# One activation-table step a group instead of two, in a fused Mamba and tree-FFN kernel on one core

## The reference

```python
h = layernorm(x) * (1 + ca) + sa
xp, z = split(h @ W_in)                     # 256 channels each
u = silu(causal_conv4(xp) + conv_b)
dt_r, Bm, Cm = split(u @ W_xp)              # 8, 16, 16
delta = softplus(dt_r @ W_dt + dt_bias)
# for each of the 16 states n:  h_t = exp(delta_t * A_n) * h_(t-1) + delta_t * B_tn * u_t
# y_t = sum over n of C_tn * h_t
y = (y + u * D_skip) * silu(z)
x = x + ga * (y @ W_out)
h = layernorm(x) * (1 + cb) + sb
gate = sigmoid((h @ Wq.T) @ routers.T)      # 255 nodes of a tree of depth 8
leaf_prob = products of gate and 1 - gate along each path   # 256 leaves
x = x + gb * ((leaf_prob @ leaf_values) @ Wout_w.T + Wout_b)
```

## Time and profile before

| | |
|---|---|
| median of 3 runs | 538.68 us (534.51 to 538.88) |
| profiled execution, its own time | 538.69 us |
| its span, first to last instruction | 536.9 us |
| outside the span | 1.79 us |
| busy: DVE, POOL, PE, ACT | 454.3, 445.3, 406.6, 374.1 us |
| granted TensorE clock, mean | 0.898 of full |

### The profile page before, as it was taken

How to read it: one execution, slowest core, us unless ns; L and a number is a source line. 1 busy time by engine, 2 the same in 40 slices (tenths; PEclk the granted TensorE clock), 3 DMA queues, 4 the chain that set the end, 5 groups by cost and what they waited for, 6 DMA issues and landing times. The chain is left out here.

```text
span 536.9 us, 6647 instructions
## 1 busy us (share of the span) xinstructions
PE 406.6 (76%) x2104; PEld 278.4 (52%) x2135; DVE 454.3 (85%) x542; ACT 374.1 (70%) x680; POOL 445.3 (83%) x246
## 2 busy tenths in 40 slices
PE   8978834896679757984899747984899758574887
PEld 4436524483548435663567435662557435464554
DVE  6788794998999968998799968997899968998871
ACT  3367774478966888588756898598856886448454
POOL 3468889999899978997799979997889978998800
PEclk8989885899799969998799979999899969785899
DMA  6491062200721073303512063303512063300001
GB/s 169 132 357 75 6 235 89 106 2 21 249 106 62 6 236 117 99 0 125 208 34 89 5 236 117 100 1 131 202 43 81 6 234 118 98 0 2 8 13 39
DMA packets 24867, 53.16 MB, mean 99 GB/s; under 512 B 4601, under 2 KB 13952, under 8 KB 20736
## 3 DMA queue, kind: packets, MB, share of 16 engines
q1 hardware_dynamic: 24832, 52.74, 29.0%
HBM read 50.11 MB, written 2.62 MB: 98 GB/s over the span
## 5 line engine op out<-in xcount | busy, mean ns | idle before, releaser
L561 POOL TENSOR_TENSOR hc<-h,c_rows 128x1024 f32<-128x1024 f32 x126 | 296.6, 2367 | 41.4 <-DVE h L1286 38.0
L1286 DVE TENSOR_TENSOR_SCAN h<-dA,state,dbu 128x512 f32<-128x512 f32 x192 | 234.6, 1270 | 20.1 <-ACT dA L649 19.8
L649 ACT ACTIVATE dA<-delta,a_neg 128x512 f32<-128x512 f32 x256 | 173.1, 684 | 44.5 <-DVE h L1286 43.6
L1065 PE MATMUL yb<-ident,hc 128*128 128x128 f32 x1024 | 155.8, 291 | 22.0 <-POOL hc L561 20.1
L1065 PEld LDWEIGHTS yb<-ident,hc 128*128 128x128 f32 x1024 | 133.3, 152 | 64.7 <-issue 32.4
L548 POOL TENSOR_TENSOR dbu<-du,b_rows 128x1024 f32<-128x1024 f32 x48 | 113.4, 2363 | 4.0 <-DMA b_rows<-bc_dram 4.0
L1299 DVE TENSOR_TENSOR dbu<-du,bb 128x1024 f32<-128x1024 f32 x80 | 96.5, 1206 | 20.5 <-PE bb L1090 10.9
L1286 DVE TENSOR_TENSOR_SCAN h<-dA,dbu 128x512 f32<-128x512 f32 x64 | 74.6, 1210 | 17.8 <-ACT dA L649 17.7
L973 PE MATMUL mf<-f_hT,w_conv 128*128 128x512 f32 x112 | 56.1, 628 | 2.0 <-ACT zu L708 1.4
L996 PE MATMUL mf<-zu,w_xdt 128*128 128x512 f32 x56 | 31.2, 640 | 17.1 <-ACT delta L742 11.5
L824 PE MATMUL mt<-ident,t_xhat 128*128 128x128 f32 x28 | 7.6, 427 | 37.8 <-ACT t_xhat L590 37.8
(11 more groups left out here) (198 smaller groups left out, 544.5 us busy)
## 6 DMA issues: line engine op xcount, KB each, us to landing
c_rows<-bc_dram SPq DMA_DIRECT2D x32, 1024.0 KB, 6.8
b_rows<-bc_dram SPq DMA_DIRECT2D x48, 256.0 KB, 7.3
xs<-in_L_attn_x_dram SPq DMA_DIRECT2D x8, 256.0 KB, 3.8
out_dram<-xs SPq DMA_DIRECT2D x7, 256.0 KB, 5.6
ygT<-in_L_attn_conv_w_dram SPq DMA_DIRECT2D x1, 512.0 KB, 5.1
bc_dram<-xd SPq DMA_DIRECT2D x8, 64.0 KB, 1.6
probT<-in_L_wmod_dram SPq DMA_DIRECT2D x1, 384.0 KB, 4.0
w_in<-in_L_attn_W_in_dram SPq DMA_DIRECT2D x1, 256.0 KB, 4.2
```

Of the source, the lines that this page charges most:

```text
L561: nc.gpsimd.tensor_tensor(hc[:, pair % RC, :, :], h[:, pair % RH, :, :], c_rows[:, q, n % NQ, :].unsqueeze(1).broadcast_to([P, HALVES, T]) ...
L649: nc.scalar.activation(dA[ke % RD][:, :], delta[:, ge % 2, half, :], ACT.Exp, scale=a_neg[:, half, n:n + 1]).then_inc(s_dA, 1)
L1065: last = nc.tensor.matmul(bank[:, tile], hc[:, pair % RC, half, tile], ident[:, :], start=False, stop=n == N - 1, is_transpose=True, skip_ ...
L1286: v.tensor_tensor_scan(h[:, pair % RH, half, :], dA[k % RD][:, :], dbu[:, pair % RW, half, :], start, ALU.mult, ALU.add).then_inc(s_scan, 1)
```

## The change

ACT has one table step a group, at F_TABLES = 10: silu table, silu of u and z, softplus table, softplus of the nodes (groups with a leaf part) and of delta, exp table. Delta's softplus reads the two products right from PSUM, with the bias, in two instructions of 512; the two copies with bias (L742) are gone. So that both products can wait to be read, the second goes to the bank `mt` (the "t" side of JOBS), between the output product and the leaf sums. Statistics of the next front come at step 12 beside those of the tail; the steps of the tail, the leaf part, du and the B parts are moved; in group 0 the tail weights are turned, multiplied and taken out by step 9.

```diff
--- before.py
+++ after.py
@@ -81,26 +81,27 @@
 
 
 
-    N_STATS, N_RSTD, N_OFF, N_XHAT = 19, 21, 22, 25
-    F_SILU, F_DT, F_SP, F_DU = 10, (13, 15), 17, (25, 26)
-    F_HI, F_R1, F_MID, F_R2, F_LO = 21, 22, 23, 24, 25
-    T_GATE, T_ADD, T_STATS, T_RSTD, T_OFF, T_XHAT = (4, 5), 12, 12, 15, 16, 19
-    U_FIN = 28
+    N_STATS, N_RSTD, N_OFF, N_XHAT = 12, 16, 17, 20
+    F_TABLES, F_DU = 10, (21, 22)
+    F_HI, F_R1, F_MID, F_R2, F_LO = 18, 19, 20, 21, 22
+    T_GATE, T_ADD, T_STATS, T_RSTD, T_OFF, T_XHAT = (4, 5), 12, 12, 13, 14, 18
+    U_FIN = 20
 
 
 
 
     JOBS = {
         "f": {("xp", 0): (1, (0, 1)), ("xp", 1): (1, (3, 4)), ("z", 0): (1, (7,)), ("z", 1): (1, (8,)),
-              ("dt", 0): (1, (11, 12)), ("dt", 1): (1, (13, 14)), ("xd", 0): (1, (15, 16)), ("tr", 0): (2, (28,))},
-        "t": {("yt", 0): (-1, (6,)), ("yt", 1): (-1, (8,)), ("out", 0): (-1, (10,)), ("tr", 0): (-1, (20,)),
-              ("lp", 0): (-2, (22,)), ("lp", 1): (-2, (24,)), ("ff", 0): (-2, (25, 26)), ("node", 0): (-1, (28,)),
-              ("node", 1): (-1, (30,))},
+              ("dt", 0): (1, (11, 12)), ("xd", 0): (1, (15, 16)), ("tr", 0): (2, (26,))},
+        "t": {("yt", 0): (-1, (6,)), ("yt", 1): (-1, (8,)), ("out", 0): (-1, (10,)), ("dt", 1): (1, (13, 14)),
+              ("lp", 0): (-2, (15,)), ("lp", 1): (-2, (17,)), ("ff", 0): (-2, (19, 20)), ("tr", 0): (-1, (22,)),
+              ("node", 0): (-1, (25,)), ("node", 1): (-1, (27,))},
     }
     BY_DVE = {"out", "ff"}
+    FIRST_BY_HAND = {("f", "xp"): 1, ("f", "dt"): 1, ("t", "dt"): 1, ("f", "xd"): 1, ("f", "tr"): 2}
     Z_OF_0 = (29, 30)
     TR_OF_1 = STEPS - 1
-    W_TURN, W_COPY, W_MUL, W_TAKE, W_SCALE = (4, 9), (7, 11), 13, 16, 20
+    W_TURN, W_COPY, W_MUL, W_TAKE, W_SCALE = (2, 5), (4, 7), 8, 9, 20
 
     WARM_START = 9
     WARM_XHAT = 3
@@ -110,8 +111,7 @@
     for side in JOBS:
         for g in range(FIRST, LAST + 1):
             for (name, part), (off, steps) in sorted(JOBS[side].items(), key=lambda job: job[1][1]):
-                first = {"xp": 1, "dt": 1, "xd": 1, "tr": 2}.get(name, 0) if side == "f" else 0
-                if first <= g + off < GROUPS:
+                if FIRST_BY_HAND.get((side, name), 0) <= g + off < GROUPS:
                     job_at[side, name, part, g + off] = len(read_at[side])
                     by = "dve" if name in BY_DVE else "act"
                     reads[side, by] = reads.get((side, by), 0) + 1
@@ -337,6 +337,13 @@
             _, by, count = read_at[side][job_at[side, name, part, g]]
             eng.wait_ge(s_read[side, by], count)
 
+        def wait_delta(eng, g, half):
+
+            if g == 0:
+                eng.wait_ge((s_d0, s_delta)[half], 1)
+            else:
+                wait_read(eng, "ft"[half], "dt", half, g)
+
         def wait_bank(eng, side, n):
 
             if n >= RM[side]:
@@ -562,7 +569,7 @@
                                                 ALU.mult).then_inc(s_hc, 1)
                     if front and s in F_DU:
                         half = F_DU.index(s)
-                        pool.wait_ge(s_delta, f + 1)
+                        wait_delta(pool, f, half)
                         pool.wait_ge(s_silu, f + 1)
                         nc.gpsimd.tensor_tensor(du[:, f % 2, half, :], delta[:, f % 2, half, :],
                                                 zu[:, f % 2, HALVES + half, :], ALU.mult).then_inc(s_du, 1)
@@ -640,7 +647,7 @@
                         ge, se = divmod(ke, STEPS)
                         n, half = divmod(se, HALVES)
                         if se < HALVES:
-                            act.wait_ge(s_delta, ge + 1)
+                            wait_delta(act, ge, se)
                         if ke >= RD:
                             act.wait_ge(s_scan, ke - RD + 1)
                         if ke == 0:
@@ -707,7 +714,7 @@
                                 act.wait_ge(s_gate, HALVES * (f - 2) + half + 1)
                             nc.scalar.activation(zu[:, f % 2, half, :], job("f", "z", half, f)[1][:, :],
                                                  ACT.Copy).then_inc(s_read["f", "act"], 1)
-                    if front and s == F_SILU:
+                    if front and s == F_TABLES:
 
                         wait_read(act, "f", "xp", 1, f)
                         u_part = zu[:, f % 2, HALVES:, :]
@@ -716,6 +723,20 @@
                             wait_read(act, "f", "z", 1, fz)
                             z_part = zu[:, fz % 2, 0:HALVES, :]
                             nc.scalar.activation(z_part, z_part, ACT.Silu).then_inc(s_zsilu, 1)
+                    if (front or leaf) and s == F_TABLES:
+                        if leaf:
+
+                            wait_read(act, "t", "node", 1, u)
+                            if u:
+                                wait_job(act, "t", "lp", 1, u - 1)
+                            nc.scalar.activation(node_s[:, :, :], node_x[:, :, :], ACT.Softplus, scale=-1.0)
+                            nc.scalar.activation(node_x[:, :, :], node_x[:, :, :], ACT.Softplus).then_inc(s_nsp, 1)
+                        if front:
+                            for half in range(HALVES):
+                                side = "ft"[half]
+                                wait_job(act, side, "dt", half, f)
+                                nc.scalar.activation(delta[:, f % 2, half, :], job(side, "dt", half, f)[1][:, :],
+                                                     ACT.Softplus, bias=dtb[:, half:half + 1]).then_inc(s_read[side, "act"], 1)
                         nc.scalar.preload_act_table_set("natural_log_exp_and_others")
                     if front and s == read_step("f", "xd", 0):
                         wait_job(act, "f", "xd", 0, f)
@@ -736,25 +757,6 @@
                         act.wait_ge(s_r2, f + 1)
                         nc.scalar.activation(b_parts[B_LO:P, f % 2, :], xd_bank[B_LO:P, :],
                                              ACT.Copy).then_inc(s_lo, 1)
-                    if front and s in F_DT:
-                        half = F_DT.index(s)
-                        wait_job(act, "f", "dt", half, f)
-                        nc.scalar.activation(delta[:, f % 2, half, :], job("f", "dt", half, f)[1][:, :], ACT.Identity,
-                                             bias=dtb[:, half:half + 1]).then_inc(s_read["f", "act"], 1)
-                    if (front or leaf) and s == F_SP:
-                        if front:
-
-                            wait_read(act, "f", "dt", 1, f)
-                            both = delta[:, f % 2, :, :]
-                            nc.scalar.activation(both, both, ACT.Softplus).then_inc(s_delta, 1)
-                        if leaf:
-
-                            wait_read(act, "t", "node", 1, u)
-                            if u:
-                                wait_job(act, "t", "lp", 1, u - 1)
-                            nc.scalar.activation(node_s[:, :, :], node_x[:, :, :], ACT.Softplus, scale=-1.0)
-                            nc.scalar.activation(node_x[:, :, :], node_x[:, :, :], ACT.Softplus).then_inc(s_nsp, 1)
-                        nc.scalar.preload_act_table_set("natural_log_exp_and_others")
                     if tail and s == T_RSTD:
                         rstd(t, t_mv, t_rs, t_nm, s_tvar, s_trs)
                     if tail and s == T_XHAT:
@@ -993,6 +995,8 @@
 
                     if piece == 0:
                         pe.wait_ge(s_silu, g + 1)
+                        if (side, g) == ("t", 1):
+                            pe.wait_ge(s_wtake, 1)
                     last = nc.tensor.matmul(bank[:, :], w_xdt[:, piece, part * P:(part + 1) * P],
                                             zu[:, g % 2, HALVES + piece, :],
                                             start=piece == 0, stop=piece == HALVES - 1)
```

## The result

The changed kernel takes 546.65 us (median of 4 runs, 545.31 to 547.69); the kernel before took 538.36 beside it (534.51 to 538.88). The ratio is 1.0168, with an interval of 1.0116 to 1.0221: slower by 1.7%, just outside the range that was forecast. The profiled execution took 547.69 us, 545.9 of them span. In what follows medians are over all executions of a kernel but one, of `two_loads`, that took 986 us.

The account below looks back on a forecast made before the run. ACT's absences in other tables set the turn, by how far each outlasts what DVE has in hand. Group 0 +7.7, group 1 +1.8, five turns -5.2, the end -4.3 sum to 0.0: 538.7 us, range 529 to 546.

Parts of the forecast that it names:

- The turns, "-5.2": Five loop turns, 138.34 to 438.24 us: 26.3 us of DVE standing against 31.5, so 5.2 us less.
- Scan 13's standing: DVE waiting at scan 13 for ACT's one long absence: 4.1 us a turn, 5.4 in group 6.
- DVE's reserve: Group 5, during ACT's absence: exps in hand, residual and statistics keep DVE busy until 360.3, scan 13 starting at 364.4.
- The second term: Step 20: a new DVE wait for the leaf product, 0.9 us a turn, between none and 2.
- The third term: Behind the absence: DVE's waits for B rows and "remote", 10.0 us in five turns, taken as gone.
- the slower rival: Steps 13 to 20: late leaf product brings B-row waits back, 548.7 us; 0.30, shared with a start-up worse than priced.
- Group 0, "+7.7": Group 0: the longer absence delays POOL, full afterwards, its multiply moving from 61.36 to 69.0: 7.7 us lost, at least 4.3.
- the 1.8 us ahead of the load: Group 0: PE's weight products and three copies, now earlier, delay the silu load by an estimated 1.8 us.
- Group 1, "+1.8": Group 1: POOL stands 3.7 us at two multiplies, where it had 1.98: 1.8 us lost, between 0 and 2.5.
- From 438.24 on, "-4.3": Group 7 on: softplus step costs nothing and DVE's waits go: 4.3 us gained, between 1.4 and 6.0.
- The 6.28 us of group 0, "worth nothing": Group 0 at 87.92: DVE's longest wait goes with the earlier offset, but gains nothing since POOL is full there.
- ACT's 16 us, "none of it on the path by itself": ACT's spared loads (9.0 us) and copies (9.4 us) gain nothing by themselves, since ACT waits for DVE in the rest of a turn.

Follow-up runs that it names:

- two_loads: The changed kernel with two more table loads in the one table step, right after silu of z (14 loads in seven groups): 556.87 us, ratio 1.0306.
- after: The changed kernel itself, with nothing further edited: 546.65 us.
- ufin22: The changed kernel with DVE adding the leaf product (leaf residual) at step 22 in place of 20: 537.23 us, ratio 0.9984.
- before: The kernel without the change, run beside each other kernel: 538.36 us beside the changed kernel.
- after_paths: The changed kernel with POOL making the path matrices at the start of the program, not at step 20 of group 0: 540.06 us, ratio 1.0025.
- split_g0: The changed kernel with the table step cut in two in group 0 alone (silu at step 10, softplus at 15): 542.93 us, ratio 1.0085.
- ufin22_ring4: The changed kernel with leaf residual at step 22, a fourth exp buffer, in SBUF, and ACT three steps ahead: 580.65 us, ratio 1.0799.

## Why the prediction was wrong

**The turns, "-5.2": the step that failed.** It had three terms. Scan 13's standing was 4 x 4.1 + 5.4 = 21.8 and measured 24.8 (4.57, 4.55, 5.08, 4.72 and 5.90). The absence has the length I gave it: the scan comes 10.47 us after the silu load, against 10.5. DVE's reserve was a little too large.

The second term was 0.9 us a turn at step 20; it measured 2.1 in four turns and 0.4 in the last, 8.9 for 4.5. In group 5 DVE comes to step 20 23.6 us after the silu load (forecast 23.5), and ACT's second leaf exp is done after 21.7 (21.5): both as forecast. Mis-sized is the way from that exp to the finished product, 2.9 us in the forecast and 4.0 measured. I had PE's work in front of the product done by then, at the full clock. But PE has stood twice, its clock is at the lower level, the leaf sum takes 2.07 and 1.91 us, and the y_sum, fill and y_sum behind it are slow too; the product starts 1.3 us after the exp is done. In the kernel before that sum, in group 5, follows other work closely:

```profile
383.53 1.13 PE L949 MATMUL mt<-node_s,path 128*128 128x512 f32 x2 [0.21 <-ACT probT L781]
384.49 1.02 PE L950 MATMUL mt<-node_x,path 128*128 128x512 f32 x2
```

The last turn of after shows the other case in the same kernel. In group 6 the clock is back before the sum ends, the rows behind it have the full pace, and DVE waits 0.44 us, 2.85 after the exp is done:

```profile
447.82 0.60 PE L1069 MATMUL yb<-ident,hc 128*128 128x128 f32 x4
448.26 0.38 PE L1094 MATMUL bb<-b_parts,sel 128*128 128x512 bf16 x1
448.47 0.60 PE L1069 MATMUL yb<-ident,hc 128*128 128x128 f32 x4
```

```profile
448.32 0.58 ACT L783 ACTIVATE probT<-mt 128x512 f32<-128x512 f32 x1
```

```profile
451.75 0.69 DVE L1333 TENSOR_TENSOR xs<-mt,xs 128x512 f32<-128x512 f32 x1 [0.44 <-PE mt L1038]
```

The third term was that the waits for B rows vanish; 3.9 us at the dbu products remain. Together 37.6 us in place of 26.3: +6.1 and not -5.2.

The rule I had written for the slower rival was the right mechanism at nearly the right price, 10 us over the sum. It said it decides "at some 2 us of lateness", and the lateness was 2.1. What made the product late was PE's clock and not ACT's second exp, and the place was another too: the time is lost mostly at the residual itself, and the fills behind lose less. `ufin22` shows it: move what waits, and the five turns take 6.7 us less than in before (293.2 for 299.9), a little more than the forecast 5.2. That this waiting also feeds itself is an argument from the rows, not tested apart: DVE stands at scan 13, so PE's work from DVE comes late and PE stands, so its sum is slow, so DVE stands again.

**Group 0, "+7.7": mechanism right, size too high.** Silu load forecast at 52.2, measured 51.26, though everything there is 1.4 us later from the start (POOL's first du at 26.74, not 25.35, with nothing of the change ahead of it). hc forecast at 65.6 and 69.0, measured 64.71 and 68.07. POOL's extra standing is 6.5 us. From the silu load to scan 13 I had 12.2 us and it is 12.15; too high was the 1.8 us ahead of the load, where 0.85 was lost, the start's 1.4 included. With the start of the profile before (`after_paths`) the change itself costs 5.3 us here, not 7.7. `split_g0` gets 3.7 back.

**Group 1, "+1.8".** 2.6 and 1.1 us were forecast for the two waits, 3.87 and 0.97 measured, 4.8 for 3.7. Both groups together: forecast 9.5 later at the first cut, measured 9.6, of which 1.4 is the start and 8.2 the change. That the two numbers agree is luck: too high in one place, too low in the other, and the start on top.

**From 438.24 on, "-4.3".** Measured -6.5 behind the cut (98.7 us before, 92.2 after), a little beyond the bound of -6.0.

**The 6.28 us of group 0, "worth nothing".** Right, and shown from two sides: with the offset earlier the wait is 6.91 or 11.77 us for POOL, and with POOL's path matrices out of the way it is gone and 7.0 us are won.

**ACT's 16 us, "none of it on the path by itself".** Right. And its reverse holds too: `two_loads` adds ACT work inside the absence and pays over half of it. The switch was priced rightly, at the load alone: the load of 374.83 is followed by its exp after 1.30 us, with no drain behind it in this trace.

What stays open: which of PE's two spells of standing brings its clock down, and what the turn would be with the clock held up. What the lower clock costs is read from the rows of groups 5 and 6, and no run changes it alone. Open too is what DVE waits for in the 3.2 us at L1303 that have no releaser.

## What to carry to other kernels

Putting two table visits into one saves loads, but here the reader of that engine's results paid for the longest absence beyond what it had in hand, not for the sum; look first for the place with the least in hand, here group 0, and leave the visits apart there. When an absence is moved or lengthened, go down the list of the engines that stood through it, and ask of each step right behind it whether its reader can come two steps later: here that was one number, and it was worth 9.4 us. A matmul priced from a busy stretch is too cheap behind an idle one; price it from a row that follows a wait.

## What the runs showed of the hardware

A scan on DVE with both large inputs in SBUF, while POOL multiplies there too, is slow. With the exps in PSUM it takes 1254 ns in the median, with the exps in SBUF 2193, up to 3423. POOL pays as well: its products for dbu take 2762 ns in the mean in place of 2362. In `ufin22`:

```profile
L555 POOL TENSOR_TENSOR dbu<-du,b_rows 128x1024 f32<-128x1024 f32 x48 | 113.4, 2362 | 4.4 <-DMA b_rows<-bc_dram 4.4
```

In `ufin22_ring4`:

```profile
L556 POOL TENSOR_TENSOR dbu<-du,b_rows 128x1024 f32<-128x1024 f32 x48 | 132.6, 2762 | 4.1 <-DMA b_rows<-bc_dram 4.1
```

That it is POOL shows where POOL stands still. From 397.36 to 398.78 it does nothing (its next multiply starts at 398.78 after a wait of 1.41 us), and the scan in that gap is as fast as from PSUM:

```profile
397.42 1.28 DVE L1291 TENSOR_TENSOR_SCAN h<-dAs,state,dbu 128x512 f32<-128x512 f32 x1
```

The scan of 138.46 lies in such a gap as well and takes 1.28. And where the scan begins first, POOL is the slower one: a scan of 1.20 us starts at 304.73, and the multiply behind it at 304.77 lasts to 308.08, 3.31 us for 2.36.

The Trainium skill ("SBUF — State Buffer", SBUF: two separate sides) says that a DVE instruction with two inputs in SBUF and a POOL instruction that reads SBUF take a pair of ports in turn, each for its whole length. The rows agree: a scan that has to wait out a whole multiply would take 1.25 + 2.36 = 3.6 us, and the slowest took 3.42. The two kernels with one exp in four in SBUF, and ACT three steps ahead, are 32 and 43 us slower than those with all in PSUM.

The other is PE's clock behind short waits. In after, behind 2.08 and 2.36 us of standing with 0.8 us of work between, the granted clock was 0.50 for the whole leaf sum, and four products took 3.98 us that take 2.04 at the full clock. In `ufin22` it was 0.50 behind the first such wait already, of 2.08 us: the fill of 371.53 took 0.61 us, the y_sum behind it 1.06.
